# Gather and one-hot buffers released by VectorE's add instead of TensorE's matmul, in two graph layers

## What is computed

```
x = layernorm(x + relu(x @ w0 + segment_sum((x @ w1)[src], dst)))           # layer 1

h_all = einsum('nf,rof->rno', x, W).reshape(8, n, 8, 32)                    # layer 2, 8 relations, 8 heads
h_src, h_dst = h_all[edge_type, src], h_all[edge_type, dst]
scores = einsum('ehd,hd->eh', h_src, attn_src) + einsum('ehd,hd->eh', h_dst, attn_dst)
scores = where(scores > 0, scores, 0.2 * scores)
amax = maximum(segment_max(scores, dst), 0.0)
w = exp(scores - amax[dst]);  w = w / (segment_sum(w, dst) + 1e-12)[dst]
out = segment_sum(h_src * w[..., None], dst)
x = layernorm(x + out)
```

## Time and profile before

| | us |
|---|---|
| median of 3 runs | 3712.33 (3709.70 to 3739.15) |
| the profiled execution | 3669.94, its span 3668.1 |
| mean granted TensorE clock, profiled | 0.828 |
| PE busy | 2651.0 (72%) |
| POOL busy | 2105.6 (57%) |
| DVE busy | 2067.8 (56%) |
| ACT busy | 1551.3 (42%) |

### The profile page before, as it was taken

The page is one execution under the profiler, slowest core; times in us unless marked ns, Lnnn a source line. Parts: engine busy times, 40 slices in busy tenths (PEclk is TensorE's granted clock), DMA queues, the critical chain, the costliest instruction groups (busy, mean ns, idle before and its releaser), DMA issues.

```text
span 3668.1 us, 41478 instructions
## 1 busy us (share of the span) xinstructions
PE 2651.0 (72%) x10903; PEld 1882.3 (51%) x10903; DVE 2067.8 (56%) x4361; ACT 1551.3 (42%) x3505; POOL 2105.6 (57%) x1854
## 2 busy tenths in 40 slices
PE   5779957777777776778999944667676776776750
PEld 4368835555555555556444423555454554554530
DVE  6966525544554444445311214677676677675778
ACT  3255434445544454444333313444444444443430
POOL 1456576666766766765000046777677777777711
PEclk9978878788888888888999966778787878787875
DMA  2400033322436323323444433333333333333313
GB/s 61 119 1 1 1 107 109 97 89 89 98 89 168 123 89 91 91 88 75 155 176 180 166 115 85 102 103 103 94 103 100 99 99 105 100 100 104 101 41 117
DMA packets 172077, 360.86 MB, mean 98 GB/s; under 512 B 43722, under 2 KB 107920, under 8 KB 165220
## 3 DMA queue, kind: packets, MB, share of 16 engines
q0 software_dynamic: 83888, 233.09, 23.0%
q1 hardware_dynamic: 80788, 71.35, 6.9%
q10 hardware_dynamic: 7200, 54.07, 3.6%
HBM read 274.80 MB, written 83.57 MB: 98 GB/s over the span
## 4 chain that ended last, share of the span: by engine, by line
PE 49%; issue 16%; another core or an unknown queue 13%; DVE 11%; ACT 5%; POOL 3%; DVEq 2%; DMA 1%; SPq 0%; POOLq 0%; ACTq 0%; PEldq 0%
PE ps L1512 20%; PE ps L1562 9%; PE ps L1623 8%; DVE nodes L657 5%; PE ps L1477 4%; PE ps L1608 3%; ACT region L1366 2%; ACT region L1373 2%; DVE nodes L775 1%; POOL region L1142 1%; PE ps L1600 1%; DVE region L764 1%; DVE region L448 1%; PE ps L1485 1%
## 5 line engine op out<-in xcount | busy, mean ns | idle before, releaser
L1192 POOL DMA_INDIRECT region<-ha_d,idx_t x880 | 980.1, 1114 | 451.2 <-issue 248.6
L1512 PE MATMUL ps<-region 128*128 128x256 f32 x3424 | 955.4, 436 | 333.9 <-DVE nodes L657 217.5
L1154 POOL DMA_INDIRECT region<-y_d,edge_z x856 | 869.2, 1015 | 396.3 <-issue 243.2
L1512 PEld LDWEIGHTS ps<-region 128*128 128x128 f32 x3424 | 706.0, 217 | 580.9 <-issue 271.5
L657 DVE TENSOR_TENSOR nodes<-ps,nodes 128x512 f32 x856 | 592.1, 692 | 659.3 <-PE ps L1512 322.2
L1623 PE MATMUL ps<-region 128*128 128x264 f32 x1760 | 608.2, 486 | 177.0 <-DVE nodes L775 87.5
L1300 ACT ACTIVATE region<-iota_n,edge_z 128x256 f32<-128x256 f32 x856 | 364.6, 496 | 614.0 <-PE ps L1512 364.7
L1623 PEld LDWEIGHTS ps<-region 128*128 128x128 f32 x1760 | 365.1, 231 | 348.2 <-DVE nodes L775 156.2
L775 DVE TENSOR_TENSOR nodes<-ps,nodes 128x264 f32 x880 | 370.0, 420 | 101.3 <-PE ps L1623 51.1
L1562 PE MATMUL ps<-region,edge_z 128*128 128x512 f32 x800 | 353.3, 595 | 0.0
L1362 ACT ACTIVATE region<-ps 128x512 f32<-128x512 f32 x220 | 131.7, 598 | 511.0 <-remote 292.6
(11 more groups left out here) (241 smaller groups left out, 2715.2 us busy)
## 6 DMA issues: line engine op xcount, KB each, us to landing
ha_d<-region ACTq DMA_DIRECT2D x50, 1056.0 KB, 4.0
region<-ha_d,idx_t POOLq DMA_INDIRECT x880
region<-y_d,edge_z POOLq DMA_INDIRECT x856
edge_z<-level_d SPq DMA_DIRECT2D x55, 136.0 KB
kl_d<-region SPq DMA_DIRECT2D x8, 903.0 KB
edge_z<-kl_d SPq DMA_DIRECT2D x55, 129.0 KB
y_d<-edge_z SPq DMA_DIRECT2D x25, 256.0 KB, 3.2
x_d<-edge_z SPq DMA_DIRECT2D x25, 256.0 KB, 4.2
```

The costliest lines, as they stand in the source:

```text
L1154: g.indirect_dma_start(rows0[c % RING][:, u, :], None, y_d, bass.IndirectOffsetOnAxis(ap=y_idx[:, k:k + 1], axis=0), bounds_check=node_bou ...
L1192: g.indirect_dma_start(rows[s][:, k, :], None, ha_rows, bass.IndirectOffsetOnAxis(ap=idx_t[:, B * b + k:B * b + k + 1], axis=0), bounds_ch ...
L1512: mm = t.matmul(ps[:, u, h * D:(h + 1) * D], lhsT=sel0[c % 4][:, u, h * P:(h + 1) * P], rhs=rows0[c % RING][:, u, :], start=True, stop=True)
```

## The change

In four places a wait for PE's count becomes a wait for DVE's. The number waited for is the same column or step in each: the four that used the slot last. In layer 2 the counts start elsewhere (`segs` at 64, `added` at 4), so the offsets differ, and where the old wait was met from the start (the first four batches of gathers, the first batch of one-hots) there is none now. A slot is thus freed when its sum has been added to the node tile, and no longer when its matmul is done. Nothing else is touched.

```diff
--- before.py
+++ after.py
@@ -1147,7 +1147,7 @@
 
             def gather_columns(c):
                 if c >= RING:
-                    g.wait_ge(segs0, 4 * (c - RING) + 4)
+                    g.wait_ge(added0, 4 * (c - RING) + 4)
                 g.sem_inc(pool_turns, 1)
                 for u in range(4):
                     k = 4 * c + u
@@ -1185,7 +1185,8 @@
 
             def gather(b, s):
                 for q in range(4):
-                    g.wait_ge(segs, B * b + 4 * q + 4)
+                    if b >= 4:
+                        g.wait_ge(added, B * (b - 4) + 4 * q + 8)
                     g.sem_inc(pool_turns, 1)
                     for u in range(4):
                         k = 4 * q + u
@@ -1295,7 +1296,7 @@
 
             def column_one_hots(c):
                 if c >= 4:
-                    a.wait_ge(segs0, 4 * (c - 4) + 4)
+                    a.wait_ge(added0, 4 * (c - 4) + 4)
                 for u in range(4):
                     last = a.activation(sel0[c % 4][:, u, :], iota_n[:, :], ACT.Abs,
                                         bias=y_local[:, 4 * c + u:4 * c + u + 1], scale=-1.0)
@@ -1369,7 +1370,8 @@
 
             def one_hots(b, q):
                 a.wait_ge(aparts, 4 * b + q + 1)
-                a.wait_ge(segs, B * b + 4 * q + 52)
+                if b:
+                    a.wait_ge(added, B * b + 4 * q - 8)
                 a.activation(sel[q].rearrange("p u e -> p (u e)"), apart[q % 2].rearrange("p u e -> p (u e)"), ACT.Relu,
                              bias=ones[:, 0:1], scale=-1.0).then_inc(sel_made, 1)
```

## The result

| | before | changed |
|---|---|---|
| median of 4 runs each, us | 3723.9 (3709.7 to 3739.2) | 3826.5 (3806.2 to 3846.2) |
| ratio, 95% interval | | 1.0315 (1.0270 to 1.0361) |
| profiled execution, us | 3669.9 | 3834.6 |
| layer 1's gathers, first to last, us | 457 to 1723 (1266) | 481 to 1817 (1336) |
| layer 2's gathers, first to last, us | 2146 to 3494 (1348) | 2244 to 3664 (1420) |

The account below looks back on a forecast made before the run. Both layers were taken as bound by POOL's gather issuing plus its pauses. Layer 1's 34 us and layer 2's 50, less 20, gave about +63 us: 3775 us from a 3712 median (profiled 3733); range 3700 to 3860.

Parts of the forecast that it names:

- the hold: Both layers: PE's news arrives late, some 10 us a cycle; back-to-back gathers make it, a roughly 2 us pause ends it.
- The price of a pause: POOL restarts later by the awaited add: layer 1 0.79 us median, 81 us; layer 2 2.4 us, 104 us.
- What is given back: Both layers: longer pauses come less often, so of the 81 and 104 us only 34 and 50 stay, 84 in sum.
- the 20 us taken off after it: Both layers: half of some 40 gaps under 1.9 us become long enough to end a hold, saving 20 us.
- model: Cycle equation giving N, gathers per cycle, from pause p: layer 1's N 15.6 to 18.2, layer 2's 18 to 25.
- Layer 2: Gathers gated on adds: 43 gaps 2.4 us longer at the median, 104 us; 50 us left after give-back.
- ACT's edits at zero: ScalarE's one-hots waiting for adds, both layers: slack 5 us in layer 1, adds ended earlier in layer 2; zero cost.
- The ring takes it all: Both layers: POOL is only ahead, so a later restart shortens a later wait; 3700 to 3730 us; 27%.
- Fewer holds: Both layers: longer pauses end or delay more holds; 3625 us; decided if pauses fall by over 30%; 17%.
- three engines waiting on one semaphore: Version of the fewer-holds rival (17%): three engines waiting on one PE semaphore slow its news; no size of its own.
- Nothing is given back: Both layers: the whole ceiling of 185 us stays; 3897 us; 10%.
- my likeliest: Both layers: part of the 185 us is given back, about +63 us, 3775 us; 46%.

Follow-up runs that it names:

- h1: Kernel before plus forced breaks in layer 1's gathers and layer 2's gathers waiting for adds, on a chip with pauses: 3840.2 us against 3644.2, ratio 1.0533.
- c1: The whole change again beside the kernel before, on another chip with pauses: 3757.7 us against 3660.8, ratio 1.0245.
- e1: Kernel before with only layer 1's gathers waiting for the adds, on a chip with pauses: 3718.0 us against 3668.3, ratio 1.0152.
- d1: Kernel before with only layer 1's gathers waiting for the adds, on a chip without pauses: 3452.9 us, ratio 0.9990.
- f1: Kernel before with only layer 2's gathers waiting for the adds, on a chip without pauses: ratio 1.0014.
- f2: Kernel before with only ScalarE's one-hots waiting for the adds, both layers, on a chip without pauses: ratio 0.9999.
- g1: Kernel before with only layer 2's gathers waiting for the adds, on another chip without pauses: ratio 1.0030.
- e2: Kernel before with PE counting by two every second column or step and VectorE waiting for pairs, on a chip with pauses: 3679.4 us, ratio 1.0026.
- f3: Kernel before, but in layer 1 POOL waits before every second group until its last group landed; chip without pauses: 3713.3 us, ratio 1.0782.
- g2: Kernel before, but in layer 1 POOL waits before every second group until its last group landed; another chip without pauses: 3724.3 us, ratio 1.0791.
- b1: Kernel before with PE counting by two every second column or step and VectorE waiting for pairs, on a chip without pauses: 3413.3 us, ratio 0.9880.

## Why the prediction was right or wrong

**What bounds the stages, and the hold.** Right. Both stages are gathers, issuing gaps and pauses, and the differences of these rows give the +70 and the +72 us. Outside the two windows the profiles stay within 5 us of each other, but for the 24 us ahead of the first gather. That the hold goes where the gathering has breaks is shown by h1; that it needs nobody on POOL or ACT to wait for PE is shown by the changed kernel, in which neither does: 449 of 856 adds are still over 2 us late (450 before). Against the Trainium skill's 26 ns for each count ("TensorE: Matmul & The Clock Gate", "The cost: per-tile semaphore tail") stand 2.3 us at the median on A and 0.22 us on B. By that rule there would be no hold, and that is what three of the seven chips show. Two things I had not seen. The hold, and with it the whole effect, is a matter of the chip. And a pause is not the only thing after which late news comes: in the earlier trace rows it comes at 2220.57, while POOL issues its first 64 gathers with no gap over 0.31 us until 2230.20.

**The price of a pause.** It held in layer 1. I had taken the old timeline and moved each restart behind the add of the column that it waited for. In the traces a long pause splits into two parts, from POOL's stop to the first add after it, and from there to POOL's restart. The first part hardly moved, 1.35 us before and 1.41 after (medians, the wait for the table left out). The second went from 0.77 to 2.39 us at the median, and from 1.29 to 2.80 us in the mean. This looks like more than the "0.79 us at the median", but that is the median over all gaps, and over the 44 long ones the same arithmetic gives 2.67 us in the mean. What decides is how many adds stand between the first one and the one that POOL wants (medians of the second part, us):

| wanted column, counted from the first add | before: pauses, second part | same add, 0.79 us after its end | after: pauses, second part |
|---|---|---|---|
| first | 10, 0.65 | 1.48 | 11, 1.48 |
| second | 20, 1.37 | 2.39 | 25, 2.39 |
| third | 14, 1.45 | 3.29 | 12, 3.84 |
| fourth | 0 | | 2, 4.19 |

When the gate hangs on PE's count, the news of the second and the third column comes some 0.7 to 0.8 us behind that of the first. When it hangs on the adds, the backlog of the hold is worked off one by one, at 0.90 us each and often more where DVE has other work between. So the price is 0.8 us where POOL wants the first column, 1.2 us for the second and 2.0 us for the third (means), 61 us over the long pauses. At POOL's stop three or four columns were summed and not yet added, in 43 of 44 cases before and 49 of 50 after. That the four banks set this depth I argue but did not test.

**What is given back.** This is the step that failed: "With p = 2.6 this gives N = 15.6, about the 16 of layer 1. With p = 2.6 + 81/70 = 3.76 it gives N = 18.2", which let 34 us of layer 1's 81 stand, and the 20 us taken off after it, of which about 12 are layer 1's by its share of the short gaps. About 22 us were left. Against A's before the pauses of layer 1 grew by 67 us on A, 56 on C and 51 on D:

| layer 1, without the table's wait | model | before, A | after, A | c1, C | e1, D |
|---|---|---|---|---|---|
| gathers for each pause | 15.6, then 18.2 | 12.4 | 14.8 | 14.5 | 14.3 |
| mean pause, us | 2.6, then 3.76 | 2.10 | 3.65 | 3.40 | 3.27 |
| long pauses | | 44 | 50 | 48 | 45 |
| gathers from one long pause to the next | | 18.2 | 15.9 | 16.8 | 17.8 |
| short pauses | | 25 | 8 | 11 | 15 |

The model took each cycle to be 15.6 gathers and a pause of 2.6 us, so 55 pauses in 856 gathers. The trace had 69 of 2.10 us. The 1.16 us for each pause had been worked out as 81/70, but in the model it was multiplied by 55, not 70: 17 of the 81 us were gone before anything was given back. The rest of the model came near on C and D: 13 to 15% fewer pauses, each 1.17 to 1.30 us longer, where it had 14% and 1.16. On A they grew by 1.55 us. But the reason for the model is not what the rows show. The pauses that went were short ones, worth 9 to 16 us in all; the long ones came after 15.9 to 17.8 gathers and not after more than the 18.2 of before. And the 20 us for short gaps that become long enough did not show: on A late adds stayed at 449, on C and D they were 427 and 435. Why a longer pause does not put off the next long one is open. POOL's gates stand every four gathers, which may hold the cycle to whole groups (16 gathers in 37 cycles of A, 38 of C and 37 of D, against 23 before); no run tests it.

**Layer 2.** Its terms were 50 us left of 104, less some 8 for the short gaps, about 42. Its pauses grew by 30 (C), 42 (h1 on G) and 55 us (A) against A's before. The size is about right, and that is luck. The mean pause grew by 0.5 us on all three (from 2.64 to 3.13, 3.13 and 3.17), not by 2.4, and the pauses rose in number, from 43 to 46, 49 and 54, where I had them fall by 10 to 25%. The price from the old timeline, 2.4 us a pause, did not come here, and why is open. The base is not sharp either: e1, which leaves layer 2 alone, has 52 pauses of 126 us on D. And 10 to 20 us on C and A are longer gathers (1126 and 1137 ns in place of 1114), a term that the sum did not have.

**The sum.** The forecast was about 22 us in layer 1 and 42 in layer 2. On A the pauses came to 67 and 55 us and the gathers to 20, together the stages' 142. So most of the miss is layer 1's: on D it is 29 us, as much as the 17 of the pause count and the 12 of the short gaps; on A it is 45, with pauses that grew more than the price. Between medians the loss is 97 us on C and 103 on A.

**ACT's edits at zero.** Nothing speaks against it: in layer 1 e1 and c1 lie 4 us apart. In layer 2 it rests on h1 beside c1 and after: 1394 without ScalarE's edit, 1387 and 1420 with it, so anything below these 33 us could hide. ScalarE's edits alone were never run on a chip with pauses. PE's waits for the ReLU of layer 1 went from 7 to 16 us in the changed kernel on A, but they are 9 us in c1 and 13 in e1, which has not this edit. ACT's idle time moved to the adds as forecast:

```profile
ACT region L1301 <- DVE nodes L657: 622.0, 178, 14.1
```

**The rivals.** *The ring takes it all* fell: layer 1's waits grew by 76 us, although POOL was 24 to 28 columns ahead of PE at its pauses after the change (25 to 28 before). By the rows the stage is gathers, gaps and pauses, so a longer pause is lost unless something is won back elsewhere, and being ahead does not change that. *Fewer holds* fell: pauses in layer 1 fell by 16%, not 30%, and their sum rose. Its version of three engines waiting on one semaphore fell too: with DVE alone waiting for PE's sums the late adds stayed. *Nothing is given back*, 185 us, is too high for any of the pairs: the stages grew by 142 us on A. The truth lies between it and my likeliest.

## What to carry to other kernels

A buffer freed by the reader's own count comes free when that news arrives, and the news of several steps can arrive close together. Freed by the next engine's count, it waits until that engine has worked through the pile. Price such an edit by the queue that stands in front of the awaited step when the waiter restarts, and not by one step: here 0.8, 1.2 or 2.0 us. And where a wait is always met, the edit is free: look first whether the waiting engine ever pauses, on more than one chip.

Before you take a give-back off such a price, feed the model of the cycle with the number and the mean of the pauses as the trace has them, and say which pauses should become fewer. A model with 55 longer pauses in place of 69 lost a fifth of the price, and the pauses that did become fewer were those that had cost little.

## What the runs showed of the hardware

**The same program, two kinds of chip.** Before: 3443 to 3452 us on B, E and F, 3644 to 3724 us on A, C, D and G; the nearest medians of the two kinds lie 5.6% apart. The mean granted TensorE clock of the profiled executions went with it: 0.86 to 0.87 where nothing pauses (d1, f1, f2, g1), 0.80 to 0.84 where it does (before, after, c1, e1, e2). f3 and g2, with breaks but without the late counts (16 of 856), have 0.83 too, so a lower mean clock does not by itself make a hold. Why the news of PE's matmuls is late on four of the chips is open, and so is whether it stays with a chip for good.

**A gather that meets L764 can take twice as long.** From d1's layer 2 (chip B):

```profile
2184.79 1.01 POOL L1192 DMA_INDIRECT region<-ha_d,idx_t  x1 [0.30 <-issue]
2186.06 1.22 DVE L764 TENSOR_TENSOR region<-region 128x1024 f32<-128x1024 f32 x1
2186.11 2.06 POOL L1192 DMA_INDIRECT region<-ha_d,idx_t  x1 [0.30 <-PE ps L1623]
...
2190.89 1.22 DVE L764 TENSOR_TENSOR region<-region 128x1024 f32<-128x1024 f32 x1
2191.10 1.89 POOL L1192 DMA_INDIRECT region<-ha_d,idx_t  x1 [0.31 <-issue]
```

A gather that starts while VectorE multiplies its 128 x 1024 tile took 1.89 and 2.06 us here in place of 1.01. In d1's layer 2 there are 167 such gathers, with a median of 1.96 us and a largest of 2.09. What counts is how much of the multiplication is left: 0.33 us left give 1.22 us, 0.61 give 1.50, 1.17 give 2.06, so such a gather ends 0.89 us after the multiplication, and one that starts in its last 0.1 us stays at 1.01. All 149 gathers over 1.3 us overlap L764, and of the 619 that do not overlap it none is over 1.21 us. VectorE's adds of layer 1, which read one operand from PSUM, do not do this: 4 of d1's 856 gathers there are over 1.3 us. The Trainium skill says as much, in "GPSIMD Engine Reference", section "1. Specifications": GpSimd shares its SBUF interface with VectorE and contends with instructions that have two SBUF inputs. The traces agree; the price, up to some 1.05 us for a meeting, is theirs. Over the 880 gathers of layer 2, those above 1.3 us cost, beyond 1.013 us each, 75 us before on A, 95 after, 140 in d1 and 93 in b1. The first two differ by the 20 us that layer 2's gathers grew by on A. From d1 to b1 they fall by 47 us, and all gathers together by 39, which is the 1.2% that counting by pairs gained on B. Why pairs make the long meetings fewer was not tested; it may be only a shift of DVE's work against POOL's.
